# A transformer block with attention and a routed FFN on one Trainium2 core: three places for the transposed expert rows, and one register load for two products

## The reference

```python
# attention without a softmax, 16 heads of 8
q, k, v = l2norm(x_n @ Wq + bq), l2norm(x_n @ Wk + bk), x_n @ Wv + bv    # x_n = layernorm(x)
x = x + ((q k^T / n**sigmoid(m)) v) @ Wo + bo
# FFN on h = layernorm(x): 16 experts, each token goes to its best one, and a shared MLP sees all
logits = h @ router_w.T
score  = sigmoid(logit of the top expert)          # 0 for the 15 others
gate, up = split((h * score) @ gate_up_proj[e])    # 128 -> 2 x 128
routed = (up * silu(gate)) @ down_proj[e]          # 128 -> 128
shared = (silu(h @ shared_gate_w.T) * (h @ shared_up_w.T)) @ shared_down_w.T   # 128 -> 512 -> 128
x = x + shared + routed
```

## Time and profile before

| | |
|---|---|
| median of three runs | 272.96 us |
| the profiled execution's own time | 275.04 us |
| its span | 273.3 us |
| PE busy | 219.1 us (80%) |
| DVE busy | 173.5 us (63%) |
| ACT busy | 135.7 us (50%) |
| POOL busy | 108.5 us (40%) |
| granted TensorE clock, mean | 0.845 of full |

### The profile page before, as it was taken

How to read it: one execution, slowest core, us unless ns; L and a number is a source line. 1 busy time by engine, 2 the same in 40 slices (tenths; PEclk the granted TensorE clock), 3 DMA queues, 4 the chain that set the end, 5 groups by cost and what they waited for, 6 DMA issues and landing times.

```text
span 273.3 us, 3732 instructions
## 1 busy us (share of the span) xinstructions
PE 219.1 (80%) x1059; PEld 171.0 (63%) x1059; DVE 173.5 (63%) x447; ACT 135.7 (50%) x265; POOL 108.5 (40%) x120
## 2 busy tenths in 40 slices
PE   0867598889898599299299556999999999999970
PEld 0325465666857488296278354888897677778740
DVE  2369899999978746245936424445546566776654
ACT  2424446758759878816135313444443556455630
POOL 6008466743756645474720000000000467675640
PEclk9995799897868755555569959999999999999998
DMA  5994238000100001001423330244123213222215
GB/s 147 319 336 151 77 116 260 1 0 1 39 13 29 19 26 35 19 29 40 149 73 104 109 97 0 67 136 121 56 79 116 59 31 86 77 47 79 77 38 154
DMA packets 33639, 23.32 MB, mean 85 GB/s; under 512 B 3154, under 2 KB 30804, under 8 KB 33620
## 3 DMA queue, kind: packets, MB, share of 16 engines
q1 hardware_dynamic: 30996, 18.69, 23.5%
q0 software_dynamic: 2048, 4.20, 5.4%
q10 hardware_dynamic: 576, 0.20, 0.3%
HBM read 13.77 MB, written 9.31 MB: 84 GB/s over the span
## 4 chain that ended last, share of the span: by engine, by line
PE 53%; DVE 19%; ACT 10%; issue 8%; POOL 4%; DMA 2%; ACTq 1%; DVEq 0%; POOLq 0%
PE quad_banks L972 9%; PE quad_banks L973 8%; PE quad_banks L974 8%; PE quad_banks L924 3%; PE bank L1009 3%; PE bank L1115 3%; PE bank L1088 3%; DVE qkv L663 3%; PE bank L1011 3%; PE bank L1010 3%; DVE ss L672 3%; DVE st L628 2%; ACT h_rows L452 2%; DMA w_qkv<-L_attn_Wv 2%; DVE xgT L854 2%
## 5 line engine op out<-in xcount | busy, mean ns | idle before, releaser
L424 POOL DMA_INDIRECT h_rows<-y_slots,gpos x32 | 32.7, 1022 | 92.4 <-DMA y_slots<-yg 75.6
L397 POOL DMA_INDIRECT x_slots<-h_rows,pos x32 | 31.6, 988 | 25.0 <-ACT h_rows L507 15.0
L740 DVE TENSOR_TENSOR s_act<-quad_banks,sg_act 128x512 f32<-128x512 f32 x32 | 22.0, 690 | 25.0 <-ACT sg_act L512 16.2
L512 ACT ACTIVATE sg_act<-quad_banks 128x512 f32<-128x512 f32 x32 | 19.1, 598 | 35.9 <-PE quad_banks L974 29.2
L924 PE MATMUL quad_banks<-w_c,xT 128*128 128x384 f32 x64 | 31.9, 661 | 0.6 <-issue 0.6
L372 POOL TENSOR_TENSOR qkv<-qkv,rn 128x512 f32<-128x512 f32 x16 | 16.9, 1074 | 32.5 <-DVE rn L680 32.5
L924 PEld LDWEIGHTS quad_banks<-w_c,xT 128*128 128x128 f32 x64 | 16.6, 272 | 13.3 <-issue 10.1
L854 DVE TENSOR_TENSOR xgT<-bank,xgT 128x512 fp32r<-128x512 f32 (+1 forms) x12 | 8.2, 680 | 25.8 <-ACT xgT L591 25.8
L518 ACT CAST s_spl<-s_act 128x512 fp32r<-128x512 f32 x32 | 19.6, 613 | 5.3 <-issue 4.8
L745 DVE TENSOR_TENSOR s_spl<-s_act,s_spl 128x512 fp32r<-128x512 f32 x32 | 21.9, 683 | 0.3
L591 ACT CAST xgT<-bank 128x512 fp32r<-128x512 f32 (+1 forms) x12 | 6.9, 576 | 27.5 <-PE quad_banks L974 23.3
(11 more groups left out here) (161 smaller groups left out, 582.2 us busy)
## 6 DMA issues: line engine op xcount, KB each, us to landing
h_rows<-x_slots SPq DMA_DIRECT2D x47, 64.0 KB, 1.9
y_slots<-yg SPq DMA_DIRECT2D x11, 256.0 KB, 2.3
xT<-L_attn_x_turned SPq DMA_DIRECT2D x8, 256.0 KB, 6.1
xres<-L_attn_x SPq DMA_DIRECT2D x8, 256.0 KB, 6.1
w_raw<-L_ffn_gate_up_proj SPq DMA_DIRECT2D x4, 512.0 KB, 5.1
out<-xres SPq DMA_DIRECT2D x8, 256.0 KB
x_slots<-zero_rows SPq DMA_DIRECT2D x16, 64.0 KB
x_slots<-zero_rows SPq DMA_DIRECT2D x1, 960.0 KB, 9.8
```

The lines of the kernel that those rows point to most:

```text
L397: g.indirect_dma_start(out=x_slots, out_offset=bass.IndirectOffsetOnAxis(ap=pos[:, t:t + 1], axis=0), in_=h_rows[:, t, :], in_offset=None) ...
L424: g.indirect_dma_start(out=h_rows[:, t, :], out_offset=None, in_=y_slots, in_offset=bass.IndirectOffsetOnAxis(ap=gpos[:, t:t + 1], axis=0) ...
L740: v.tensor_tensor(s_act[:, k % 2], pair[:, 2 * (k % 2) + 1], sg_act[:, k % 2], ALU.mult).then_inc(s_act_rdy, 1)
```

## The change

The tile `xgT` gets a third place (`XRING = 3`). `x_hi(q)` and `x_lo(q)` write into place `q % 3`, the gate and up products read from it, and the wait is for `gate_up(q - 3)` in place of `gate_up(q - 2)`, from q = 3 on. Apart from that, `gate_up_experts(q)` keeps the registers that it loaded, and `down_experts(q)`, two steps later, uses them and loads none of its own.

```diff
+    XRING = 3
-        xgT = sb("xgT", [P, 2, 2, Q * P], F32R)
+        xgT = sb("xgT", [P, XRING, 2, Q * P], F32R)
             def x_hi(q):
                 n = len(windows(q)) * P
                 act.wait_ge(gT_mm, q + 1)
-                if q >= 2:
-                    act.wait_ge(e_gu_mm, q - 1)
-                a.copy(xgT[:, q % 2, 0, 0:n], ps_gT[:, 0:n]).then_inc(gT_hi, 1)
+                if q >= XRING:
+                    act.wait_ge(e_gu_mm, q - XRING + 1)
+                a.copy(xgT[:, q % XRING, 0, 0:n], ps_gT[:, 0:n]).then_inc(gT_hi, 1)
...
             def x_lo(q):
                 n = len(windows(q)) * P
                 dve.wait_ge(gT_hi, q + 1)
-                if q >= 2:
-                    dve.wait_ge(e_gu_mm, q - 1)
-                v.tensor_tensor(xgT[:, q % 2, 1, 0:n], ps_gT[:, 0:n], xgT[:, q % 2, 0, 0:n].bitcast(F32), ALU.subtract
+                if q >= XRING:
+                    dve.wait_ge(e_gu_mm, q - XRING + 1)
+                r = q % XRING
+                v.tensor_tensor(xgT[:, r, 1, 0:n], ps_gT[:, 0:n], xgT[:, r, 0, 0:n].bitcast(F32), ALU.subtract
                                 ).then_inc(gT_sb, 1)
...
+            expert_of = {}
+
             def gate_up_experts(q):
                 experts = window_experts(q, mybir.EngineType.PE)
+                expert_of[q] = experts
                 pe.wait_ge(gT_sb, q + 1)
                 if q >= 2:
                     pe.wait_ge(e_act_rdy, q - 1)
                 for j, n in enumerate(windows(q)):
-                    last = split_product(gate_up_banks(q % 2)[:, j, :], xgT[:, q % 2, :, P * j:P * j + P],
+                    last = split_product(gate_up_banks(q % 2)[:, j, :], xgT[:, q % XRING, :, P * j:P * j + P],
                                          gu_cols[:, :, bass.ds(experts[j] * 2, F2)])
...
             def down_experts(q):
-                experts = window_experts(q, mybir.EngineType.PE)
+                experts = expert_of[q]
```

## The result

The changed kernel takes 263.29 us, the median of six runs (261.05 to 265.3), against 272.68 us before (six runs). The ratio is 0.9647, with a 95% interval of 0.9589 to 0.9706: 9.6 us faster, 8.0 to 11.2. It is formed from the mean times, without the run of 265.3 us, which was over 1.5% above the fastest. I had forecast 265.4 us, 7.6 us less than before, and a range that began at 263.9. The direction and the mechanism were right; the size was too small.

The account below looks back on a forecast made before the run. PE was taken as the bound, held in the experts' stage by a closed loop over `xgT`'s second place. Gains of 2.90 + 4.37 + 0.3 = 7.6 us off 272.96 gave 265.4 us, range 263.9 to 268.8.

Parts of the forecast that it names:

- the term of steps 2 to 9: Experts' stage: eight steps shorten from 3.85 to 3.30 us, 26.29 us in place of 30.66, a gain of 4.37 us.
- the term for the time before `turn_x(2)`: Start of the kernel up to `turn_x(2)`: nothing changes there, a gain of 0.
- The loop, and that the third place opens it: Experts' stage: the second place of `xgT` closes a 3.85 us loop; a third leaves PE alone setting 3.30 us steps.
- The start of the stage: `turn_x(2)` to `turn_x(4)`: `turn_x(3)` starts right behind `gate_up(0)`, clock rising at 164.93, a gain of 2.90 us.
- rival D: Start of the stage: the clock rises two or three microseconds later, costing 2.8 us; 268.2 us, chance 0.07.
- The registers: PE's sequencer: 12 of 24 loads go, gaining 0.3 us in front of the weights of `down(10)`.
- Rival A: Steps with `turn_x`: the sequencer stays on the path, 0.63 us between transposes and products remains; 267.0 us, chance 0.18.
- Behind the stage: After the experts' stage: gathers and PE's shared MLP move by the same amount, so nothing is given back.
- Rivals B and C: Experts' stage. B: another wait takes over the loop, 269.8 us, chance 0.08. C: five half-clock steps, 279.4 us, chance 0.05.

Follow-up runs that it names:

- e3: The changed kernel itself, run once more on another occasion; ratio to the kernel before 0.9665.
- e6: The changed kernel with four places of `xgT` in place of three; one run, stage 37.58 us from `turn_x(2)` to `down(10)`.
- e8: The changed kernel with the stage's first three transposes in three PSUM banks and issued earlier; 256.63 us, ratio to the kernel before 0.9424.
- e1: The changed kernel with the down products loading their own registers again (third place alone, 24 loads); ratio to the kernel before 0.973.
- e2: The changed kernel with `xgT` back at two places (kept registers alone, 12 loads); ratio to the kernel before 0.9993.
- e9: The changed kernel with two places and the load for `gate_up(1)` to `gate_up(9)` moved in front of the held `turn_x`'s wait; ratio to the kernel before 0.984.
- e7: The kernel before, with transposed rows going through two PSUM banks in turn from `turn_x(3)` on; ratio to the kernel before 0.9762.
- e4: The kernel before, with `xgT` given room for three places but using two; ratio to the kernel before 0.9988.
- e11: The changed kernel with four register loads a step, all used (48 in all); one run, 272.91 us against 273.75 of the kernel before.
- e5: The changed kernel with down loading again, plus an unused load before `turn_act` that was not in the program that ran; one run, stage 39.03 us.

## Why the prediction fell outside its range, and what in it was right

- **What failed: the term of steps 2 to 9, which was mis-sized.** The sum gave these steps a gain of 4.37 us, from a step of 3.30 us. They gained 5.29 us, with a step of 3.18. I took 3.30 us from step 10 of the kernel before (2.87 us) plus 0.43 for four transposes. The second part was right: a step with `turn_x` took 0.44 us more than one without (3.18 and 2.74, after). The first part was not. I had written that in steps 10 and 11 "PE showed no gap although the loads stood there", and took them as the array's own pace. But the array can do this step in 2.74 us (after, e3, e6, e8). The 0.13 us lie in gate and up (1.53 for 1.49) and from down to the next products (0.91 for 0.82). A start that comes 0.1 us late, behind an instruction whose duration reaches over it, shows no idle time. What makes such a start late is the load in front of the products, when the sequencer comes to it late: with three places the same distance is 0.82 us with one load a step, and 1.06 with two (e1). For the 0.91 us of the kernel before this cause is read from its trace and not shown by a run: the two-place kernels with one load were slower still (e2, e9). In all, steps 2 to 9 came out 0.92 us shorter than the 26.29 forecast, most of the 1.1 us by which the stage's sum fell short.
- **What failed besides: nothing was allowed for what lies outside the stage.** The stage's 8.7 us alone would take 272.96 to 264.3, inside the range. The median lies 9.7 us under the one on record, 1 us more than the stage gave, and the term for the time before `turn_x(2)` was zero. In the profile 1.95 us lie there. No run ties them to the change.
- **The loop, and that the third place opens it: right.** Steps went from 3.85 us to a step that PE's array alone sets. e6 shows that the place is then no bound, e2 that without it nothing opens. The prediction named the place as what closes the loop; e7 shows that it takes two links, and that the single bank is the other.
- **The start of the stage: right**, 3.00 us for 2.90, with the clock rising as far behind `turn_x(2)` as before. That this is partly luck is shown by e3: the rise came later (6.87 us for 5.96), so rival D's late rise happened there, at a third of its price, and not for the reason that D gives. The kernels with two places have it too (e4, e9).
- **The registers: right in one place, and a second place missed.** I gave them 0.3 us in front of `down(10)`. The stage of e1 against that of the changed kernel gives 38.11 - 37.59 = 0.52 us.
- **Rival A** did not occur in the steps with `turn_x`: the products followed the transposes by 0.36 us, not 0.63, with 12 loads and with 24 (e1).
- **Behind the stage: right.** `down(10)` to the end took 65.86 to 66.06 us in all thirteen profiles, that of the kernel before among them.
- **The range: too narrow on the lower side.** It took the scatter of three runs (1.6 us) for the scatter of the time. The six runs of the changed kernel lie 4.3 us apart, and `turn_x(2)` started anywhere between 154.9 and 161.1 us in the twelve profiles with the same start of the stage. The sum of the stage, 8.7 us, lies within the measured 8.0 to 11.2.
- **Rivals B and C** did not occur: the smallest time to spare was 1.2 us (1.3 forecast), and no stretch of half clock began in the changed kernel's stage after the rise at 163.0.

What stays open: why the first half scatters by 6 us; why the clock falls before `turn_x(1)` in some executions and behind it in others; why a load takes 0.33 us at one place and over 0.6 at another; why step 10 took 2.99 us in e2 and 3.00 in e9; and whether any of the 1.95 us before the stage is the change's.

## What to carry to other kernels

A stage that is "busy" can still be a closed loop: follow what releases each engine through one step, and compare start to start with a stretch where nothing holds the engine. Check that such a stretch is itself not set by something else, the instruction stream's own pace above all, before you multiply its length by the number of steps. A loop can hang on two buffers at once, here the tile's place and the PSUM bank, and then one more of either opens it. A register load belongs in front of the wait, where the engine stands idle anyway.

## What the runs showed of the hardware

- A register load on PE's sequencer costs nothing in the trace as long as the sequencer is ahead of the array. With 12 or 24 loads (after, e1) the steps were the same 3.18 us, with 48 (e11) they were 3.92 to 4.09. Behind a held instruction one load cost 0.26 us a step (e2 and e9).
- Such a load, of four values, took 327 ns at the least (e5) and 747 ns at the most (e1). Its median was 336 ns with 24 loads (before) and 513 ns with 12 (after).
- Four transposes took 0.36 us when gate and up followed and 0.44 when down followed, at the same clock (after, step 5). In e8 eight transposes of the rows took 0.88 us, 0.44 for four, when other transposes followed. So the same group takes longer or shorter by what stands around it.
- The clock rose 3.9 us after the start of `turn_x(2)` in one execution of the same kernel and 5.9 us in another (after and e3), with PE busy throughout in both. In the first it had fallen before `turn_x(1)` (at about 156.2 us), in the second behind it (at about 158.4), both times while PE stood waiting for DVE. In e8, without these waits, it did not fall there.
